# One table of jobs for every engine and the DMA queue, from the second score product to the end

## What is computed

```python
x = L0_attn_hidden_states
x = _layernorm(x + _L0_attn_ref(x, Wq, Wk, Wv, Wo))      # q,k,v = x@W; softmax(q k' * s + band mask) @ v; @ Wo
x = _layernorm(x + _L0_ffn_ref(x, w_router, ...))        # top_k rows -> attention -> silu(gate)*up -> down -> back
```

## Time and profile before

| what | value |
|---|---|
| median of the runs | 1341.29 us |
| the profiled execution's own time | 1338.84 us |
| its span, first to last instruction | 1336.7 us |
| mean granted TensorE clock | 0.984 |
| PE busy, share of the span | 91% |
| DVE, ACT, POOL busy | 67%, 46%, 38% |
| packets of the DMA queue, share of 16 engines' span | 40.4% |

### The profile page before, as it was taken

How to read it: one execution, slowest core, us unless ns; L and a number is a source line. 1 busy time by engine, 2 the same in 40 slices (tenths; PEclk the granted TensorE clock), 3 DMA queues, 4 the chain that set the end, 5 groups by cost and what they waited for, 6 DMA issues and landing times.

```text
span 1336.7 us, 19528 instructions
## 1 busy us (share of the span) xinstructions
PE 1221.1 (91%) x6770; PEld 1038.4 (78%) x6770; DVE 899.6 (67%) x2483; ACT 612.2 (46%) x1449; POOL 514.0 (38%) x468
## 2 busy tenths in 40 slices
...
GB/s 165 98 62 95 60 91 60 91 60 91 60 91 59 91 100 139 68 127 109 142 62 77 77 82 87 83 69 89 65 93 61 101 238 88 190 94 172 195 179 94
DMA packets 250868, 135.55 MB, mean 101 GB/s; under 512 B 191681, under 2 KB 224449, under 8 KB 250769
## 3 DMA queue, kind: packets, MB, share of 16 engines
q1 hardware_dynamic: 250352, 132.99, 40.4%
...
...
## 4 chain that ended last, share of the span: by engine, by line
PE 38%; DVE 30%; ACT 13%; issue 9%; POOL 7%; DMA 3%; POOLq 0%; SPq 0%; ACTq 0%; DVEq 0%
PE proj L1228 20%; DVE arena L1754 7%; ACT arena L1531 5%; DVE prob L1805 5%; PE y L1228 5%; DVE prob L1803 5%; PE o L1228 5%; ACT s L1570 4%; PE s L1228 3%; DVE s L1789 3%; DMA turned<-prob 3%; POOL arena L2107 2%; POOL arena L2117 2%; DVE yacc L1840 2%; ACT tp L1570 2%
## 5 line engine op out<-in xcount | busy, mean ns | idle before, releaser
L1228 PE MATMUL proj<-arena 128*128 128x256 f32 (+1 forms) x3504 | 651.2, 335 | 25.7 <-DVE arena L1754 23.8
L1228 PEld LDWEIGHTS proj<-arena 128*128 128x128 f32 x3504 | 536.1, 190 | 100.0 <-DVE arena L1754 39.6
L2117 POOL TENSOR_SCALAR arena<-turned 128x384 fp32r<-128x384 f16 (+1 forms) x256 | 279.7, 1099 | 409.6 <-DMA turned<-prob 378.6
L1754 DVE TENSOR_TENSOR arena<-proj,arena 128x512 fp32r<-128x512 f32 (+1 forms) x256 | 139.2, 555 | 223.8 <-ACT arena L1531 223.7
L2107 POOL TENSOR_TENSOR arena<-wraw,arena 128x1024 fp32r<-128x1024 f32 x73 | 174.6, 2398 | 205.8 <-ACT arena L1531 205.7
L1228 PE MATMUL y<-arena 128*128 128x512 f32 x816 | 217.4, 402 | 11.0 <-DVE yacc L1840 9.0
L1570 ACT ACTIVATE s<-s,stat 128x384 f32<-128x384 f32 (+1 forms) x171 | 90.2, 527 | 278.6 <-DVE stat L1789 271.9
L1228 PE MATMUL o<-arena 128*128 128x256 f32 (+2 forms) x966 | 179.1, 306 | 42.3 <-POOL arena L2117 35.2
L1228 PEld LDWEIGHTS o<-arena 128*128 128x128 f32 x966 | 148.0, 191 | 57.5 <-issue 15.1
L1228 PEld LDWEIGHTS y<-arena 128*128 128x128 f32 x816 | 148.4, 191 | 44.5 <-DVE yacc L1840 16.2
L1531 ACT ACTIVATE arena<-proj 128x512 fp32r<-128x512 f32 (+1 forms) x256 | 122.0, 486 | 130.8 <-PE proj L1228 86.7
...
## 6 DMA issues: line engine op xcount, KB each, us to landing
...
turned<-prob SPq DMA_TRANSPOSE x256, 2.8
...
```

What stands on the lines that cost most here:

```text
L1228: ins = e.matmul(out_ap, l[a], r[b], start=first and i == 0 and j == 0, stop=final and i == n - 1 and j == 2, skip_group_check=skip)
L1754: e.tensor_tensor(dst_lo, src, dst_hi.bitcast(F32), ALU.subtract).then_inc(*V_.inc(*name, "lo"))
L2117: e.tensor_scalar(strided(pT[1], js[0] * 3 * P + (i - js[0] + 1) * P, 2 * P, n, P), tT[i % 2][:, n:2 * n, :], 1.0 / PROB_SCALE, None, ALU. ...
```

## The change

Both tables go. One table `JOBS` takes their place. It begins at `scores.0.1`, the second score product of the program, and names every job of every engine to the end. What is planned, which instructions a job makes, the buffers and the banks are the same, and each engine has exactly the same jobs as before: only their order within each of the five lists is new. Of TensorE's 1201 jobs that issue something, 686 can be left in place with the rest moved around them, of DVE's 1216, 681, of ACT's 1111, 607, of POOL's 372, 309, and of the DMA queue's 454, 348. The mean shift of a job is 2.0 places on TensorE, 4.1 on DVE, 2.7 on ACT and 1.0 on POOL.

```diff
-CHANGE_HEAD = ("scores", 15, 0)
-CHANGE = """
...
+JOBS_HEAD = ("scores", 0, 1)
+JOBS = """
+D.xload.1.0 D.xload.1.1 D.xload.1.2 D.xload.1.3 D.xload.1.4 D.xload.1.5 D.wload.5 T.scores.0.1 T.qkfirst.0.q.1 T.v.0.1
+V.scores.0.1 D.tp.0.0 S.finend.1 S.scores.0.1 T.finrow.0 T.qk.0.k.1 S.v.0.1 V.norm.0.1 D.wload.6 T.qk.0.q.1 S.qk.0.k.1
...
+S.qk.6.k.1 V.qk.6.k.1 T.pv.5.5 S.v.3.4 T.scores.6.0 V.v.3.4 T.scores.6.1 V.scores.6.0 T.scores.6.2 V.scores.6.1
+S.scores.6.0 T.v.3.5 V.norm.6.0 S.scores.6.1 T.pv.5.6 V.norm.6.1 D.tp.6.0 S.v.3.5 T.scores.6.3 T.qkfirst.6.q.1 V.v.3.5
+D.tp.6.1 V.scores.6.2 T.v.3.6 V.scores.6.3 S.scores.6.2 G.tp.6.0 S.tp.6.0 V.norm.6.2 S.scores.6.3 T.out.2.0 S.v.3.6
+G.tp.6.1 S.tp.6.1 V.norm.6.3 D.tp.6.2 T.qk.6.q.1 V.v.3.6 D.tp.6.3 V.out.2.0 T.v.3.7 S.qk.6.q.1 V.qk.6.q.1 G.tp.6.2
+S.tp.6.2 T.out.2.1 S.wsplit.16.G G.tp.6.3 S.tp.6.3 T.pv.5.7 V.out.2.1 T.scores.6.4 S.v.3.7 G.wsplit.16.G S.o.5.1
+T.qkfirst.7.q.0 V.v.3.7 V.scores.6.4 V.o.5.1 S.scores.6.4 T.qk.7.q.0 V.norm.6.4 D.wload.19 T.pv.6.0 S.qk.7.q.0
...
+T.qk.31.q.1 D.tp.31.2 V.out.14.4 T.pv.30.7 D.hload.0 S.qk.31.q.1 T.out.14.5 D.hload.1 S.o.30.1 V.qk.31.q.1 D.hload.2
+S.wsplit.66.G V.o.30.1 D.hload.3 T.scores.31.3 D.hload.4 V.out.14.5 G.tp.31.1 D.hload.5 S.tp.31.1 T.scores.31.4
+V.scores.31.3 D.hload.6 S.tp.31.2 T.out.14.6 D.hload.7 G.wsplit.66.G V.scores.31.4 S.scores.31.3 S.scores.31.4
+V.norm.31.3 T.pv.31.0 T.scores.31.5 T.rinh.0 V.out.14.6 G.tp.31.2 D.tp.31.3 T.scores.31.6 V.scores.31.5 T.out.14.7
+V.norm.31.4 D.wload.69 S.scores.31.5 T.pv.31.1 S.ubias V.scores.31.6 D.tp.31.4 T.scores.31.7 S.wsplit.67.G V.out.14.7
...
-LAST_HEAD = ("scores", 31, 0)
-LAST = """
...
-S.scores.31.2 T.scores.31.3 V.rin.0 T.qk.31.q.1 S.rin.0 V.norm.31.2 G.rin.0 T.pv.30.6 D.hload.0 S.qk.31.q.1 D.hload.1
-D.hload.2 D.hload.3 D.hload.4 T.pv.30.7 D.hload.5 D.hload.6 D.hload.7 G.tp.31.0 S.tp.31.0 T.out.14.6 S.wsplit.66.G
-V.qk.31.q.1 D.tp.31.2 S.o.30.1 G.wsplit.66.G V.scores.31.3 T.scores.31.4 S.tp.31.1 T.scores.31.5 V.out.14.6
...
-        for head, table in ((CHANGE_HEAD, CHANGE), (LAST_HEAD, LAST)):
+        for head, table in ((JOBS_HEAD, JOBS),):
```

More of the change, by code:

```diff
@@ new lines @@
+T.qk.19.k.1 D.tp.18.7 T.pv.18.4 S.qk.19.k.1 T.rows.0.0 S.wsplit.41.G V.qk.19.k.1 T.out.8.4 G.tp.18.6 S.tp.18.6
+G.wsplit.41.G S.o.18.0 T.pv.18.5 V.out.8.4 S.rows.0.0 T.scores.19.0 S.tp.18.7 V.o.18.0 T.scores.19.1 T.rows.0.1
+V.scores.19.0 T.out.8.5 S.rows.0.1 V.scores.19.1 S.scores.19.0 G.tp.18.7 D.wload.44 V.count.0.0.0 S.scores.19.1
+V.count.0.1.before T.pv.18.6 V.count.0.1.0 V.out.8.5 T.pv.18.7 T.scores.19.2 V.tie.0.0 S.o.18.1 V.norm.19.0
+T.qkfirst.19.q.1 V.norm.19.1 D.tp.19.0 T.out.8.6 V.scores.19.2 D.tp.19.1 T.qk.19.q.1 V.o.18.1 S.scores.19.2 V.tie.0.1
@@ new lines @@
+V.out.8.6 G.tp.19.0 S.tp.19.0 T.scores.19.3 V.norm.19.2 S.qk.19.q.1 T.out.8.7 S.wsplit.42.G G.tp.19.1 V.count.0.0.1
+D.tp.19.2 S.tp.19.1 T.v.10.0 V.scores.19.3 S.wsplit.43.G G.wsplit.42.G V.count.0.1.1 V.qk.19.q.1 S.scores.19.3
+T.pv.19.0 V.count.0.2.before T.qkfirst.20.q.0 S.v.10.0 V.norm.19.3 S.tp.19.2 G.tp.19.2 D.wload.45 T.qk.20.q.0
+V.count.0.2.1 D.tp.19.3 G.wsplit.43.G V.v.10.0 V.out.8.7 T.pv.19.1 S.qk.20.q.0 V.count.0.3.before T.scores.19.4
+V.count.0.3.1 V.tie.0.2 T.scores.19.5 V.tie.0.3 V.scores.19.4 T.v.10.1 D.wload.46 V.scores.19.5 S.scores.19.4
@@ new lines @@
+D.tp.20.4 T.v.10.7 S.qk.21.q.0 V.qk.21.q.0 T.pv.20.0 S.v.10.7 T.scores.20.5 S.wsplit.44.G V.v.10.7 T.pv.20.1 G.tp.20.4
+V.scores.20.5 T.out.9.1 S.tp.20.4 S.scores.20.5 G.wsplit.44.G V.norm.20.5 T.scores.20.6 T.rows.0.2 T.qkfirst.21.k.0
+S.rows.0.2 V.scores.20.6 D.tp.20.5 V.count.0.0.2 S.scores.20.6 T.qk.21.k.0 V.out.9.1 D.wload.47 V.norm.20.6 T.pv.20.2
+S.qk.21.k.0 T.pv.20.3 G.tp.20.5 S.tp.20.5 V.count.0.1.2 D.tp.20.6 V.qk.21.k.0 T.scores.20.7 T.out.9.2 V.count.0.2.2
+V.count.0.3.2 V.count.0.4.before T.scores.21.0 V.out.9.2 T.qkfirst.21.k.1 V.scores.20.7 G.tp.20.6 S.tp.20.6
```

546 lines of the change are left out of this document (395 added, 151 removed).

## The result

The changed kernel takes 1233.61 us (median of 4 runs, 1232.05 to 1235.29) against 1340.93 us before: ratio 0.9201, 95% interval 0.9185 to 0.9217. The profiled execution took 1232.36 us, its span is 1230.2.

What follows compares the result with a forecast made beforehand. PE bounds the kernel, busy 91% of the span, so only its waits can go. Gains 33 + 4 + 5 + 2 + 1 = 45 us: 1338.8 - 45 = 1293.8, plus 2.45 to the median, 1296.3 us; range 1272 to 1332 us.

Steps and rivals of the forecast that it cites:

- plain groups: Some 11 repeating groups, 74 to 504 and 752 to 1049 us: loss falls from 5.5 to 2.5 us each, 33 us won.
- the walk: New lists followed through head 6 and half of head 7: about 1.0 us lost a group instead of 5.5.
- the first rival: The hand-followed loss of 1.0 us a group holds everywhere: 71 us won, 1270 us; chance 0.15.
- requests met by 0.2 us: In head 6, pv.6.4 asks at 25.8 and has its transposition at 25.6; a late landing would cost time there.
- The counts of close requests: Heads 2 to 13, requests with little PE work before them: projections under 2.6 us 37 to 17 of 48, out 39 to 16.
- 60 us stand to be won, and no more: Limit of the gain in 727 us of repeating groups: 11 groups times 5.5 us of PE waits.
- the gap at head 15: PE stood still 4.2 us until a transposition landed; with x loads and weight loads moved, 4 us won, between 0 and 5.
- the two gaps of the earlier trace: In head 31 PE waited 3.8 and 10.2 us for transposed weights; of 14 us, 5 won, bounds 0 and 12.
- rin.0: Job on DVE and POOL in head 31's chain, moved to head 22; shares in the 5 us forecast for head 31.
- The 6 us of the prediction: At the start, time the six early x loads need; through before the first transposition, so costed at nothing, at most 6 us.
- Slower rival: The chain of the weights delays the 30 pv with under 9 us of work before them: 1356 us; chance 0.08.
- PE's busy time itself changes: Sign that the prediction is wrong: PE's busy time, taken as the same before and after, changes with the order.

Runs made afterwards that it cites:

- the doubled turns: POOL's part of every transposition done twice: in the kernel before 1383.88 us (ratio 1.0314), in the changed kernel 1310.73 us (0.9778 to the kernel before).
- new_from_head31: Order of the kernel before up to the first score product of head 31, the new order from there on: 1317.59 us, ratio 0.9837.

## Why the prediction was wrong

Of the 62 us that the sum of 45 us lacks, 19 lie in the plain groups, 16 in heads 14 to 20, 18 in head 31 and 9 at the two ends.

**Plain groups, 33 us forecast, 51.6 measured.** The step that failed is the discount from the walk to 2.5 us a group. The walk had 1.0 us left per group over 60.6. Measured are 61.5 - 60.6 = 0.9, so the first rival was right here (4.5 us a group, measured 4.7, or 4.5 by the estimate for equal work). I paid 1.5 us a group, 16.5 in all, for late landings and "requests met by 0.2 us". The thin spare is real, by the doubled turns. But in the trace hardly anything is late. Landings after, as the earlier trace rows, and the whole wait of `pv` for POOL in six groups:

```profile
DMA to landing us min/median/max: 2.4/2.8/8.9
```

```profile
PE o L1497 <- POOL arena L2386: 1.7, 3, 1.3
```

A spare is no cost; what uses it up must be shown first. (The waits of the view in the earlier trace rows add up to 5.7 us, not 5.5, which changes nothing here.)

**The counts of close requests** pointed the right way, but do not carry the sum: 37 to 0 won nothing in the old order. (A later count of `out` gives 42 of 47 before and 18 after, not 39 and 16.) What came true was the walk, which took all lists together; it covered one head and a half of the 22 heads that it stands for, so that it held on average in all of them is partly luck: single heads of the new order take from 25.6 to 36.9 us.

**Heads 14 to 20, 6 us forecast, 22.1 measured.** "60 us stand to be won, and no more" held for 727 us of the program. The 248 us of heads 14 to 20 I priced by two named waits alone, the gap at head 15 and the earlier trace rows. A window over the whole stretch would have shown the budget. The step that failed is that everything but the named waits was put at nothing. Before, and below it after:

```profile
468.40:716.50 248.10, 226.34 (x1261) 197.72 (x1260) 179.96 (x509) 118.86 (x282) 111.12 (x118) 0.98 0.45 104
```

```profile
439.20:665.20 226.00, 218.78 (x1257) 193.87 (x1257) 180.05 (x503) 120.41 (x279) 108.90 (x117) 1.00 0.47 105
```

PE stood still for 21.8 us there, and for 7.2 after. Waits of this stretch, first before, then after:

```profile
PE o L1228 <- POOL arena L2117: 11.1, 6, 4.2
PEld o L1228 <- ACT works L1633: 6.8, 3, 3.3
```

```profile
PE o L1497 <- POOL arena L2386: 2.0, 2, 1.5
```

`pv` waited for POOL six times, 11.1 us in all, where the prediction had counted one wait of 4.2. Which moved jobs ended them was not tested. No 4 us gap near head 15 remains, as forecast, but not for the x loads' sake, and what PE had waited for was not the landing but the split in front of the turned weights.

**Head 31, 5 us forecast, 23.3 measured.** The step that failed is the cap of the gain at the two gaps of the earlier trace rows, 14 us. The stretch had 88.0 - 60.7 = 27.3 us of idle PE, and the clock:

```profile
1048.00:1136.00 88.00, 60.70 (x226) 42.71 (x225) 51.10 (x149) 23.79 (x55) 32.12 (x49) 0.83 0.55 155
```

After, 64.4 - 56.2 = 8.2 us are idle, and the busy time is 4.5 us less for 232 matmuls instead of 226, at a granted clock of 0.95. The transposition ahead of the loads is right in its place (9.7 us in the new order), the cause ahead of it, a split in front of turned weights, I had not read, and `rin.0` was no cause.

**Start and tail.** 4.9 us against 1 and 4.7 against 0 ± 4. The first transposition is still issued at 22.6 us, as forecast, so the six early loads held nothing up. But it was close: they took 7.6 to 8.5 us each from issue to landing, and the last, issued at 15.3, landed at 22.9. The 6 us of the prediction left out that a weight load was still on its way until 18.8. Timeline of the DMA queue after, against the earlier trace rows:

```profile
11.81 3.90 SPq L2481 DMA_DIRECT2D works<-in_L_attn_hidden_states  x6
...
22.64 1.31 SPq L2475 DMA_TRANSPOSE turned<-prob  x1
```

By the ring order in the Trainium skill ("DMA: Bandwidth & Descriptors", section "Queues, rings and completion order") the sum would have been 6 us worse only if they reached past that point. The trace shows that the last one did, by 0.3 us, and that the transposition landed 2.5 us after its issue all the same. The gain of the start was not taken apart; that of the tail comes with the order from head 31 on (new_from_head31 has it), and which job makes it is open.

**Slower rival.** The chain of the weights was to take PE's place where `pv` has under 9 us. The wait of `pv` for POOL fell from 35.2 to 5.3 us over the program. The price I took for it, 10 us where 7.3 suffices, rests on a misread row: the 5.08 us of the earlier trace rows are two issues of 1.2 to 1.3 us each, at 503.28 and 507.17, with SP waiting in between, and not one transposition held for 5.1. The second landed 4.4 us after its issue, against the median of 2.8.

**Busy time.** I had named "PE's busy time itself changes" as a sign of being wrong. It fell by 32 us and is part of the same gain: in heads 2 to 13, 17.5 of 24.3 us are idle time and 6.8 busy time. The other sign, a gain from behind head 31, is met with 4.7 us.
